# Fetching 83 of 3126 gather chunks as single rows from SyncE and ScalarE, in a two-convolution graph kernel

## The reference, cut to what matters

```python
def _gcn_conv(x, W, b, src, dst, n):
    h = x @ W
    deg = jax.ops.segment_sum(ones, dst, num_segments=n)
    dinv = jnp.where(deg > 0, jax.lax.rsqrt(deg), 0.0)
    norm = dinv[src] * dinv[dst]
    msgs = h[src] * norm[:, None]
    out = jax.ops.segment_sum(msgs, dst, num_segments=n)
    return out + b
...
h = x @ W_pre + b_pre
h = _gcn_conv(h, W1, b1, src, dst, n)
h = jax.nn.relu(h)
h = _gcn_conv(h, W2, b2, src, dst, n)
h = jax.nn.relu(h)
y = h @ W_post + b_post
```

## Time and profile before

| | |
|---|---|
| runs | 4140.93, 4140.42, 4136.22 us |
| median | 4140.42 us |
| span of the profiled execution | 4132.4 us (the page gives no other time of it) |
| instructions | 36624 |
| granted PE clock, mean | 0.879 |

### The profile page before, as it was taken

How to read it: one execution, slowest core, us unless ns; L and a number is a source line. 1 busy time by engine, 2 the same in 40 slices (tenths; PEclk the granted TensorE clock), 3 DMA queues, 4 the chain that set the end, 5 groups by cost and what they waited for, 6 DMA issues and landing times.

```text
span 4132.4 us, 36624 instructions
## 1 busy us (share of the span) xinstructions
PE 3066.6 (74%) x12107; PEld 1945.3 (47%) x12107; DVE 1279.2 (31%) x2593; ACT 392.7 (10%) x1088; POOL 3025.7 (73%) x3173
## 2 busy tenths in 40 slices
PE   6677777777776777777777777777778877777778
PEld 6344444443443443344444554444445555555556
DVE  8222222222222222222222233332224444434456
ACT  7000000000000000000001111111111111111112
POOL 3677777777777777777767777777777777777773
PEclk9878888888889888888879889999998899999988
DMA  8444444444444444444434444443334444444455
GB/s 268 135 118 118 118 119 119 118 119 120 119 118 119 118 121 118 119 119 118 121 100 119 119 118 121 118 118 112 113 113 120 117 118 118 115 121 129 118 153 176
DMA packets 248738, 513.99 MB, mean 124 GB/s; under 512 B 62491, under 2 KB 141832, under 8 KB 248296
## 3 DMA queue, kind: packets, MB, share of 16 engines
q0 software_dynamic: 150048, 410.73, 35.6%
q1 hardware_dynamic: 98504, 100.82, 8.2%
HBM read 471.70 MB, written 39.64 MB: 124 GB/s over the span
## 4 chain that ended last, share of the span: by engine, by line
POOL 66%; issue 22%; DMA 5%; PE 4%; DVE 1%; ACT 1%; SPq 0%; POOLq 0%; DVEq 0%
POOL sb_big L956 66%; DMA sb_big<-T,sb_srci 4%; PE bank L1241 2%; PE bank L570 1%; PE bank L1728 0%; ACT sb_big L791 0%; PE bank L1703 0%; PE bank L1713 0%; DVE sb_big L857 0%; DMA T<-sb_big 0%; PE bank L550 0%; DVE sb_big L859 0%; DMA sb_work<-dstT 0%; POOL sb_X L1900 0%; DVE sb_looks L668 0%
## 5 line engine op out<-in xcount | busy, mean ns | idle before, releaser
L956 POOL DMA_INDIRECT sb_big<-T,sb_srci x3126 | 2960.4, 947 | 975.9 <-issue 943.3
L1241 PE MATMUL bank<-sb_big 128*128 (+2 forms) x7056 | 2511.2, 463 | 987.8 <-DMA sb_big<-T,sb_srci 938.1
L1241 PEld LDWEIGHTS bank<-sb_big 128*128 128x128 f32 x7056 | 1303.3, 216 | 1954.6 <-issue 1816.3
L1001 DVE SCALAR_TENSOR_TENSOR sb_big<-sb_dstf,bank 128x2304 f32<-128x2304 f32 x196 | 499.0, 2546 | 29.9 <-issue 29.8
L1031 DVE SCALAR_TENSOR_TENSOR sb_work<-sb_bW,sb_work,bank 128x256 f32<-128x256 f32 x98 | 47.2, 481 | 1292.3 <-PE bank L1168 1292.3
L1016 DVE TENSOR_TENSOR sb_work<-bank,sb_work 128x257 f32<-128x257 f32 (+1 forms) x196 | 83.2, 425 | 461.3 <-PE bank L1241 461.3
L1040 DVE SCALAR_TENSOR_TENSOR sb_work<-bank,sb_dinv,sb_b 128x256 f32<-128x256 f32 x98 | 47.4, 484 | 529.3 <-PE bank L1168 529.3
L1070 ACT COPY sb_work<-bank 128x256 f32<-128x256 f32 x196 | 73.0, 373 | 1263.9 <-PE bank L1129 1263.9
L1050 DVE TENSOR_TENSOR sb_X<-sb_X,bank 128x256 f32<-128x256 f32 x98 | 41.2, 421 | 390.2 <-PE bank L1181 390.2
L1079 ACT ACTIVATE sb_work<-sb_work,sb_dinv 128x256 f32<-128x256 f32 x98 | 49.9, 509 | 878.4 <-DVE sb_work L1032 878.4
L1128 PE MATMUL bank<-sb_ident,sb_work 128*128 128x128 f32 x392 | 118.7, 303 | 16.9 <-DVE sb_work L1040 11.9
(11 more groups left out here) (200 smaller groups left out, 1719.7 us busy)
## 6 DMA issues: line engine op xcount, KB each, us to landing
sb_big<-T,sb_srci POOLq DMA_INDIRECT x3126, 2.8
sb_work<-T SPq DMA_DIRECT2D x49, 257.0 KB
T<-sb_work SPq DMA_DIRECT2D x49, 256.0 KB, 2.4
sb_work<-T SPq DMA_DIRECT2D x49, 256.0 KB
sb_X<-x SPq DMA_DIRECT2D x13, 896.0 KB, 11.1
out<-sb_X SPq DMA_DIRECT2D x9, 1024.0 KB
T<-sb_big SPq DMA_DIRECT2D x8, 899.5 KB, 6.0
sb_looks<-LO SPq DMA_DIRECT2D x23, 256.0 KB
```

Of the source, the lines that this page charges most:

```text
L956: pool.indirect_dma_start(out, None, table, bass.IndirectOffsetOnAxis(idx, 0)).then_inc(s.g[u % NSEM], 16)
L1001: v.scalar_tensor_tensor(t.S[:, b * K:(b + 1) * K, :], t.dstf[:, bass.ds(tj, K)].unsqueeze(2).to_broadcast([P, K, P]), float(-P * j), psum ...
L1241: mm = pe.matmul(ps.A[b][:, 0:w], t.S[:, b * K + k, :], rhs, start=(k == 0), stop=(k == K - 1))
```

## The change

**Skipped chunks.** `lane_tables` picks 54 chunks of convolution 1 and 29 of convolution 2. POOL leaves them out. The ring shrinks from 44 to 40 slots; the four freed ones become lanes in front of it.

**Row fetches.** For each of the 128 rows of such a chunk a plain DMA brings one row from the table to one partition of a lane; its byte offset comes from a register. In convolution 1 SyncE fetches rows 0 to 72 of a chunk, 43 rows per tile, and ACT rows 73 to 127, 32 rows per tile (10 between `act_sum` and `act_hidden`, 22 after). In convolution 2 SyncE fetches all 128, 43 per tile. The registers are loaded from SBUF, up to 32 at a time.

**Lane copy.** ACT waits for all rows of a lane in `act_sum` and copies the lane to the chunk's ring slot. PE waits for that copy in place of the gather.

**Lists.** The row numbers of those chunks come as two extra inputs; SyncE loads them, DVE multiplies them by the row's size in bytes.

The diff, cut to its core:

```diff
-RING = 44
+RING = 40
+LANES = 4
+SLOTS_ALL = RING + LANES
...
+ROW_RATES = ((73, 55, (43, 32), 24), (P, 0, (43, 1), 24))
+ACT_PARTS = ((10, 22), (0, 0, 0))
+LAST_COPY = (94, 87)
+REGS_A_LOAD = 32
...
+def lane_tables():
+    lists, steps, copies, e0 = [], [], [], 0
+    for c in range(2):
+        sp, act, per, delta = ROW_RATES[c]
+        rows, at, n = [], [], 0
+        while True:
+            last = max(ceil((n + 1) * sp / per[0]), ceil((n + 1) * act / per[1]) + 1 if act else 0)
+            e = P // 8 * (last + 1) + delta
+            if last > LAST_COPY[c]:
+                break
+            rows.append(e)
+            at.append(last)
+            n += 1
+        lists.append(rows)
+        copies.append(at)
+        for eng, (lo, hi) in enumerate(((0, sp), (sp, P))):
+            step = [[] for _ in range(NT)]
+            for r in range(len(rows) * (hi - lo)):
+                step[r // per[eng]].append((r // (hi - lo), lo + r % (hi - lo)))
+            steps.append(step)
+    return lists, steps, copies
...
+def chunk_wait(eng, s, u):
+    if u in LANE_OF:
+        eng.wait_ge(s.copied, LANE_OF[u] + 1)
+    else:
+        eng.wait_ge(s.g[u % NSEM], landed(u))
...
+def lane_rows(eng, t, s, a, which, c, j, part=None):
...
+    while todo:
+        n, p = todo[0]
+        m = next((k for k, (q, _) in enumerate(todo) if q != n), len(todo))
+        m = min(m, REGS_A_LOAD)
+        u = n + len(LANE_CHUNKS[0]) * c
+        if u >= LANES:
+            eng.wait_ge(s.copied, u - LANES + 1)
+        regs = [eng.alloc_register(f"lane{which}_{c}_{n}_{p + k}") for k in range(m)]
+        eng.reg_load(regs, t.offsets[c][LIST0 + n:LIST0 + n + 1, p:p + m])
+        for k in range(m):
+            at = eng.snap(regs[k], donate=True, min_val=0, max_val=4 * w * (N - 1))
+            eng.dma_start(t.lane[p + k:p + k + 1, u % LANES, 0:w].bitcast(U8),
+                          flat[bass.ds(at, 4 * w)].unsqueeze(0)).then_inc(s.rows[c][u % LANES], 16)
+        todo = todo[m:]
+
+def act_lane(act, t, s, i):
+    c, j = divmod(i, NT)
...
+            act.wait_ge(s.rows[c][u % LANES], 16 * P * (u // LANES + 1 - first))
+            act.wait_ge(s.agg, released(c * ET + e - RING))
+            act.copy(t.ring[:, (c * ET + e + OFF) % RING, 0:w], t.lane[:, u % LANES, 0:w]).then_inc(s.copied, 1)
+
+def dve_offsets(v, ch, t, s):
+    v.wait_ge(s.listed, 32)
+    for c, w in enumerate((TW, D)):
+        lists = t.offsets[c][LIST0:LIST0 + len(LANE_CHUNKS[c])]
+        v.tensor_scalar(lists, lists, 4 * w, None, ALU.mult).then_inc(s.scaled, 1)
...
 def pool_conv(pool, t, s, a, c):
     for u in range(c * ET, (c + 1) * ET):
+        if u in LANE_OF:
+            continue
...
     act.copy(t.YT[:, i % 2, :], ps.T[:, 0:D]).then_inc(s.TC, 1)
+    if fast:
+        act_lane(act, t, s, i)
...
-            gather_wait(pe, s, c * ET + seen)
+            chunk_wait(pe, s, c * ET + seen)
...
         act_sum(act, t, s, ps, i, True)
+        lane_rows(act, t, s, a, 1, 0, i, 0)
         act_hidden(act, t, s, ps, i, True)
+        lane_rows(act, t, s, a, 1, 0, i, 1)
...
         if b and j + 1 < NT:
             load(j + 1)
+        if fast and c == 0:
+            if j == 0:
+                sp_low(sp, t, s, a)
+                sp.wait_ge(s.scaled, 2)
+            lane_rows(sp, t, s, a, 0, c, j)
...
                 sp_looks(sp, t, s, a, j + 2)
+                lane_rows(sp, t, s, a, 0, c, j)
...
+                sp.dma_start(t.offsets[0][LIST0:LIST0 + len(LANE_CHUNKS[0])], a.srcS1).then_inc(s.listed, 16)
+                sp.dma_start(t.offsets[1][LIST0:LIST0 + len(LANE_CHUNKS[1])], a.srcS2).then_inc(s.listed, 16)
```

More of the change, by code:

```diff
@@ L13 @@
 I32 = mybir.dt.int32
+U8 = mybir.dt.uint8
 BF16 = mybir.dt.bfloat16
@@ L190, in views @@
     t.X = sb("X", [P, NT, D])
-    big = sb("big", [P, RING * TW + 2 * K * P])
+    big = sb("big", [P, SLOTS_ALL * TW + 2 * K * P])
     t.srci = sb("srci", [P, ET + 1], I32)
@@ L203, in views @@
     t.bp = sb("bp", [P, D])
-    t.onesr = sb("onesr", [1, P])
+    ones = sb("ones", [P, P])
+    t.onesr = ones[0:1, :]
     t.onesc = sb("onesc", [P, 1])
@@ L217, in views @@
     work = sb("work", [P, WORK])
-    t.ring, _ = take(big, 0, [RING, TW])
-    t.ring3, _ = take(big, 0, [RING * TW // XW, XW])
-    t.S, _ = take(big, RING * TW, [2 * K, P])
+    t.lane, o = take(big, 0, [LANES, TW])
+    t.ring, _ = take(big, o, [RING, TW])
+    t.slots, _ = take(big, 0, [SLOTS_ALL, TW])
+    t.ring3, _ = take(big, 0, [SLOTS_ALL * TW // XW, XW])
+    t.S, _ = take(big, SLOTS_ALL * TW, [2 * K, P])
     o = 0
@@ L232, in views @@
     t.OH = [v, u] * (NOH // 2 - 1) + [v, w]
-    assert last <= STAGE_SLOT[2] * TW and (STAGE_SLOT[2] + GROUP) * TW <= RING * TW - SPILL
+    assert last <= STAGE_SLOT[2] * TW and (STAGE_SLOT[2] + GROUP) * TW <= SLOTS_ALL * TW - SPILL
     t.bpx, _ = take(looks, 0, [2 * P])
-    assert o <= RING * TW - SPILL, o
+    assert o <= SLOTS_ALL * TW - SPILL, o
     t.loi = t.srci[:, :].rearrange("p (t i) -> p t i", t=2)
@@ L244, in views @@
             t.junk.append(v[:, k * P:(k + 1) * P].bitcast(BF16))
-    o = RING * TW - SPILL
+    o = SLOTS_ALL * TW - SPILL
     t.lob, o = take(big, o, [2, NPAIR], BF16)
@@ L263, in views @@
     t.rowi, _ = take(looks, 1000, [100], I32)
-    assert o <= RING * TW + 2 * K * P, o
+    assert o <= SLOTS_ALL * TW + 2 * K * P, o
     o = 0
@@ L272, in views @@
     t.zero7, o = take(big, o, [P], BF16)
-    assert o <= RING * TW, o
+    assert o <= SLOTS_ALL * TW, o
     o = 0
@@ L306, in views @@
     t.stage = [staged[:, k, :].rearrange("p (j d) -> p j d", d=TW) for k in range(2)]
-    t.stage += [t.ring[:, k:k + GROUP, :] for k in STAGE_SLOT[2:]]
+    t.stage += [t.slots[:, k:k + GROUP, :] for k in STAGE_SLOT[2:]]
     o = 0
@@ L322, in views @@
     t.lowb, o = take(looks, o, [2, P], BF16)
+    scaled, o = take(looks, o, [P], I32)
+    t.offsets = [scaled, ones[:, :].bitcast(I32)]
     t.alf, o = take(t.Wc[:, :, :].rearrange("p c d -> p (c d)"), 0, [NT, 4])
@@ L339, in views @@
     t.prodd, o = take(big, o, [2, 512])
-    assert o <= RING * TW, o
-    t.maskd, o = take(big, RING * TW, [NT * PD])
+    assert o <= SLOTS_ALL * TW, o
+    t.maskd, o = take(big, SLOTS_ALL * TW, [NT * PD])
     t.same32, o = take(big, o, [NT, WIN], BF16)
-    assert o <= RING * TW + K * P
-    t.M, o = take(big, RING * TW + K * P, [4, BATCH * P])
-    assert o <= RING * TW + 2 * K * P
+    assert o <= SLOTS_ALL * TW + K * P
+    t.M, o = take(big, SLOTS_ALL * TW + K * P, [4, BATCH * P])
+    assert o <= SLOTS_ALL * TW + 2 * K * P
     t.MT, o = take(work, 0, [4, BATCH * P])
@@ L466, in semaphores @@
     s.fput = [s.fput0, s.fput1]
+    s.rows = [[s.fg0, s.fg1, s.fcur0, s.fcur1], [sem(f"rows{k}") for k in range(LANES)]]
+    s.copied, s.scaled, s.listed = s.fput0, s.fput1, s.fin
     return s
@@ new lines, with first_need @@
+LANE_CHUNKS, LANE_STEPS, LANE_COPIES = lane_tables()
+LANE_OF = {c * ET + e: sum(map(len, LANE_CHUNKS[:c])) + n for c in range(2) for n, e in enumerate(LANE_CHUNKS[c])}
+LIST0 = 64
+assert max(map(len, LANE_CHUNKS)) <= min(P - LIST0, 15 * LANES)
+def first_need(c, e):
+    return next((j, k) for j in range(NT) for k in range(K) if min(UB[j] + k, ET - 1) >= e)
+for c, (rows, at) in enumerate(zip(LANE_CHUNKS, LANE_COPIES)):
+    for e, j in zip(rows, at):
+        assert released(c * ET + e - RING) <= NTH * (c * NT + j + 1), (c, e, j)
+        assert first_need(c, e) > (j + 1, PLACE1[0] + 1), (c, e, j, first_need(c, e))
@@ new lines, in landed @@
+def landed(u):
+    return 16 * sum(1 for v in range(u % NSEM, u + 1, NSEM) if v not in LANE_OF)
+def chunk_wait(eng, s, u):
[4 more added lines that the diff above has]
+def lane_rows(eng, t, s, a, which, c, j, part=None):
+    table, w = ((a.T1, TW), (a.T2, D))[c]
+    flat = table.rearrange("n d -> (n d)").bitcast(U8)
+    todo = LANE_STEPS[2 * c + which][j]
+    if part is not None:
+        todo = todo[sum(ACT_PARTS[c][:part]):sum(ACT_PARTS[c][:part + 1])]
+    while todo:
[12 more added lines that the diff above has]
+        todo = todo[m:]
@@ new lines, in act_lane @@
+def act_lane(act, t, s, i):
+    c, j = divmod(i, NT)
+    w = (TW, D)[c]
+    for e, at in zip(LANE_CHUNKS[c], LANE_COPIES[c]):
+        if at == j:
+            u = LANE_OF[c * ET + e]
+            first = sum(1 for v in range(u % LANES, len(LANE_CHUNKS[0]), LANES)) if c else 0
+            act.wait_ge(s.rows[c][u % LANES], 16 * P * (u // LANES + 1 - first))
+            act.wait_ge(s.agg, released(c * ET + e - RING))
+            act.copy(t.ring[:, (c * ET + e + OFF) % RING, 0:w], t.lane[:, u % LANES, 0:w]).then_inc(s.copied, 1)
@@ L1304, in dve_fast @@
     dve_onehot(v, ch, t, s, ps, 1)
+    dve_offsets(v, ch, t, s)
     for i in range(NT):
@@ L1342, in dve_fast2, with act_fast, act_fast2 @@
     dve_end(v, ch, t, s, ps)
-def act_fast(act, t, s, ps):
+def act_fast(act, t, s, ps, a):
     for i in range(NT):
         act_sum(act, t, s, ps, i, True)
+        lane_rows(act, t, s, a, 1, 0, i, 0)
```

(22 more changed lines are left out.)

## The result

The change made the kernel slower: 4435.5 us median (4434.4 to 4443.9) against 4140.2, a ratio of 1.072 with a 95% interval of 1.071 to 1.074. The forecast was 4037.

The account below looks back on a forecast made before the run. POOL's gathers, one after another, were taken to bound the kernel. Skipped chunks save 67.6 + 36.3 = 103.9 us, so 4140.4 - 103.9 = 4036.5, say 4037 us; range 4030 to 4130.

Parts of the forecast that it names:

- What bounds the kernel, and what a skipped chunk is worth: POOL's back-to-back gathers bound both convolutions; skipping 54 and 29 chunks at about 1.25 us each saves 103.9 us.
- The step that decides: Row engines must finish a tile's share in POOL's new 19.30 and 19.61 us, or everything goes at SyncE's pace.
- A row, 0.36 us: Price of one single-row DMA on SyncE and ScalarE, taken near the one-partition row, bounds 0.33 and 0.51 us.
- A register load, 1.4 us whatever the number: Price of each load on SyncE and ScalarE, bounds 1.1 and 1.8 us; the number of registers matters little.
- the sum: SyncE's time per tile from rows, register loads and the rest: 19.04 us in convolution 1, 18.8 in 2.
- Rival A: Slower: SyncE's row pitch above 0.383 us makes SyncE the bound in both convolutions; 4481 us at 0.43; chance 0.12.
- Rival B, one generator: Slower: SyncE and ScalarE take turns at one descriptor generator in convolution 1, 21.75 us per tile; 4262 us; chance 0.09.
- Rival C, gathers that stretch: Faster but less: POOL's gathers stretch beside row traffic (4067 us), or SyncE slightly misses its pace (4073); chance 0.17.
- ScalarE: Its share in convolution 1 takes 14.8 us of 19.30 per tile, with rows fitting two idle stretches of ACT.
- Ring of 40: Shrinking POOL's ring from 44 slots costs nothing; POOL stalls only if PE lags by 15 chunks, 19 us.
- Moved steps on SyncE: T2 store and own-rows load, delayed by rows, cost nothing: about 17 and some 16 us of cover remain.

Follow-up runs that it names:

- e5: The changed kernel with its own 83 chunks and rows, each register load started at the multiple of four at or below its first row: 4039.1 us.
- e4: The changed kernel with no chunk fetched by rows, all 3126 by POOL, ring of 40: 4139.1 us, ratio 1.0004 to the kernel before.
- e1: The changed kernel with rates set so each register load begins at a multiple of four rows and has a multiple of four registers: 4037.5 us.
- e2: The aligned kernel e1 with the lists of offsets one word further in SBUF, so every register load is misaligned: 4742.2 us.

## Why the prediction was wrong, step by step

- **What bounds the kernel, and what a skipped chunk is worth: right.** e5 gives back 99 us of the 103.9.
- **The step that decides: right.** "The row engines must finish their share of a tile in that time", or everything goes at SyncE's pace. It went at SyncE's pace: 21.88 us from Y to Y, above the 20.03 that the prediction named as its sign of being wrong, and with hardly a wait for Y left.
- **A row, 0.36 us: too dear.** It is 0.322 on SyncE and 0.304 on ScalarE, near the one-partition row.
- **A register load, 1.4 us whatever the number: the step that failed.** The mean is 3.3 us on SyncE (1290.9 us over 391 loads), 7.0 and 7.5 us per tile against 3.2 and 2.9 in the sum. These 3.8 and 4.6 us more turned 19.04 and 18.8 into 21.9 and 22.3; the cheaper rows gave back 1.6 us, and own-rows load, store and gaps took 1.1 where 0.4 was put down. The mistake was one of reading: the earlier trace rows show idle time behind a load and not the load, DVE 1.1 us on average where its own loads of seven registers last 1.63 (median, line 1220 before), and sixteen registers at 1.2 us beside seven at 1.4 were read as "the number matters little", where they meant that one kind of load is aligned and the other is not. The duration of these loads could be read from the trace directly. The sum didn't even use the bound that it gave itself: with 1.8 us per load a tile is 43 x 0.36 + 2.26 x 1.8 + 0.4 = 19.9 us, over POOL's 19.30, and none of the rivals is built on the load's price.
- **The figure of the Trainium skill, "DMA: Bandwidth & Descriptors", section "Latency and other measured facts", 0.6 us for a register load:** a single register took 0.46 to 0.55 us here, a little under that floor, and the measurement decides; for more than one register the floor says nothing of the cost, and the prediction didn't use it for its sum. Another page gives a rate: the Trainium skill, "Runtime: NRT & Kernel Launch", section "Instruction fetch mechanics", has about 200 ns per register, even in bulk, for the runtime's own register loads from HBM. The loads here come from SBUF; the misaligned ones take about the same (0.21 us), the aligned ones, four for 0.23, don't.
- **Rival A: its mechanism, not its cause.** SyncE was the bound in both convolutions, but with 0.322 us per row and slow loads, not with a row above 0.383. That its 4481 us lies near the measured 4435.5 is luck. Its chance of 0.12 was too low for a margin of 0.26 us in 19.3 with two unseen prices.
- **Rival B, one generator: no sign of it.** SyncE's row DMA has a median of 228 ns in convolution 1, beside ScalarE's rows, and 228 in convolution 2 without them (means 232.3 and 231.1). Of SyncE's rows in convolution 1, the 2198 that overlap one of ScalarE's take 232.6 ns on average, the 1744 others 232.0. The rule that the generator is locked for one issuer, of the Trainium skill, "Perfetto Trace Analysis", section "DMA Instruction — HWDGE (DVE, Sync)", is not contradicted by this, but at this rate no wait for it shows.
- **Rival C, gathers that stretch: no.** A gather's mean is 947 ns with and without 10,624 row DMAs in the kernel.
- **ScalarE:** its own loads take 6.8 us per tile, so its share is 32 x 0.304 + 6.8 + 1.1 = 17.6 us and not 14.8. That is below SyncE's, but the 22 rows behind the activation no longer fit into the 11.1 us before the next copy (the copy waits for ACT's own issue 87 times, 11.4 us on average, up to 12.7), and PE's weights wait 790 us for it. It didn't set the pace: SyncE waits for ACT 7.8 us from 300 to 2150 us. Whether ScalarE's slow loads alone, beside a mended SyncE, would cost time was not run, since e5 mends both engines' loads at once.
- **Ring of 40: right** (e4). **Moved steps on SyncE:** they cost nothing that shows in e5; in the changed kernel their cover was gone, and DVE waited 640 us for own rows.

## What to carry to other kernels

An issuing engine has a budget of its own: count its register loads by registers, not by loads, start them at 16-byte boundaries in groups of four, and see that some of the budget stays free (SyncE waited for 4% of the time in e5, which was enough), because a queue that misses its pace turns a gain of 2.4% into a loss of 7.2%. Before pricing an operation from the idle time around it, ask the trace for its own duration: sequencer instructions have one, though they don't count as busy. With that, single-row fetches at register addresses cost 0.32 us each on SyncE and can take work off a saturated GpSimd.

## What the runs showed of the hardware that was not expected

- A load of 32 registers from SBUF takes 2.1 us from a place in its row that is a multiple of 16 bytes and 6.9 us from any other (medians, the changed kernel); one word of offset cost the whole kernel 705 us (e1 and e2).
- 7654 single-row DMAs from SyncE and 2970 from ScalarE ran beside the gathers, and the mean of a gather stayed at 947 ns.
